# Attention on one core: the values matmuls between a transpose and a run of scores go behind the run

## What is computed

```python
cq = rms_norm(hidden_states @ w_qa.T, q_a_ln_w)
q = (cq @ w_qb.T)            # per head: 128 numbers, and 64 more with a rotary embedding
ckv_l = rms_norm(ckv[..., :KVLR], kv_a_ln_w)
scores = jnp.einsum('bhqd,bhkd->bhqk', q_full, k_full) * scale
scores = jnp.where(causal, -jnp.inf, scores)
attn = jax.nn.softmax(scores.astype(jnp.float32), axis=-1)
out = jnp.einsum('bhqk,bhkd->bhqd', attn, v)
return out @ w_o.T
```

## Time and profile before

| | before |
|---|---|
| median of 3 runs | 1726.22 us (1725.79 to 1726.46) |
| the profiled execution, its time | 1726.31 us |
| its span | 1724.6 us |
| attention loop in it | 99.4 to 1262 us |
| PE busy | 91% of the span |
| DVE busy | 69% |
| ACT busy | 59% |
| mean granted clock of PE | 0.972 of full speed |

### The profile page before, as it was taken

How to read it: one execution, slowest core, us unless ns; L and a number is a source line. 1 busy time by engine, 2 the same in 40 slices (tenths; PEclk the granted TensorE clock), 3 DMA queues, 4 the chain that set the end, 5 groups by cost and what they waited for, 6 DMA issues and landing times. The chain is left out here.

```text
span 1724.6 us, 38029 instructions
## 1 busy us (share of the span) xinstructions
PE 1571.8 (91%) x14452; PEld 1328.2 (77%) x14452; DVE 1184.3 (69%) x2472; ACT 1021.2 (59%) x2009; POOL 307.3 (18%) x752
## 2 busy tenths in 40 slices
PE   5679999999999899999999999999938999988997
PEld 3458877788888778888888888888826878866886
DVE  3347777777777677788778778778755547476564
ACT  2336665666666566667667667667624455555573
POOL 4411111112111211121211121121010002020231
PEclk8789999999999999999999999999968999999999
DMA  7000000000000000000000000000012100000000
GB/s 217 1 1 2 2 2 1 2 2 1 2 2 2 2 2 2 1 2 2 2 2 2 2 2 2 2 2 2 2 40 73 49 1 1 1 28 13 1 25 25
DMA packets 27524, 22.47 MB, mean 13 GB/s; under 512 B 9660, under 2 KB 25148, under 8 KB 27220
## 3 DMA queue, kind: packets, MB, share of 16 engines
q1 hardware_dynamic: 27348, 20.05, 4.1%
HBM read 17.95 MB, written 2.10 MB: 12 GB/s over the span
## 5 line engine op out<-in xcount | busy, mean ns | idle before, releaser
L783 ACT ACTIVATE pT_hi<-pT 128x512 f16<-128x512 f32 (+3 forms) x640 | 341.5, 534 | 303.6 <-PE pT L701 302.2
L904 DVE TENSOR_TENSOR pT_lo<-pT,pT_hi 128x512 f16<-128x512 f32 (+3 forms) x640 | 387.8, 607 | 148.5 <-ACT pT_hi L783 141.6
L772 ACT ACTIVATE pr<-pS,nmx 128x512 f32<-128x512 f32 (+3 forms) x640 | 401.0, 627 | 25.8 <-DVE nmx L895 24.0
L892 DVE TENSOR_REDUCE cmx<-pS 128x1 f32<-128x512 f32 x576 | 339.2, 617 | 64.0 <-PE pS L688 59.0
L701 PE MATMUL pT<-ident,pr 128*128 128x128 f32 x2176 | 347.3, 276 | 16.4 <-DVE pT_lo L904 15.1
L701 PEld LDWEIGHTS pT<-ident,pr 128*128 128x128 f32 x2176 | 251.9, 140 | 48.7 <-ACT pr L772 24.5
L743 PE MATMUL pO<-c_hi,pT_hi 128*128 128x65 f16 x2176 | 265.6, 194 | 18.5 <-DVE O L922 17.8
L683 PE MATMUL pS<-lT_hi,qT_hi 128*128 128x512 f32 (+2 forms) x640 | 265.5, 415 | 3.1 <-ACT pr L772 3.1
L744 PE MATMUL pO<-c_lo,pT_hi 128*128 128x65 f16 x2176 | 266.4, 193 | 0.0
L745 PE MATMUL pO<-c_hi,pT_lo 128*128 128x65 f16 x2176 | 263.7, 192 | 0.0
L688 PE MATMUL pS<-lT_hi,qT_lo 128*128 128x512 f32 (+2 forms) x640 | 255.8, 400 | 0.0
(11 more groups left out here) (268 smaller groups left out, 2484.6 us busy)
## 6 DMA issues: line engine op xcount, KB each, us to landing
X<-in_x SPq DMA_DIRECT2D x4, 512.0 KB, 6.8
wo<-in_w_o SPq DMA_DIRECT2D x1, 2048.0 KB, 10.9
out<-X SPq DMA_DIRECT2D x8, 256.0 KB, 2.0
raw<-in_wd SPq DMA_DIRECT2D x14, 128.0 KB, 2.1
raw<-in_wg SPq DMA_DIRECT2D x13, 128.0 KB, 2.7
raw<-in_wu SPq DMA_DIRECT2D x13, 128.0 KB, 2.7
wqn<-in_w_qn SPq DMA_DIRECT2D x1, 1536.0 KB, 16.1
raw<-in_qg SPq DMA_DIRECT2D x6, 128.0 KB, 2.5
```

Source lines behind the costliest of these rows:

```text
L772: act.activation(pr[:, at % RING, 0:n * P], pS[at % 4][:, 0:n * P], ACT.Exp, bias=nmx[:, p % 4:p % 4 + 1]).then_inc(sem("exped"), 1)
L783: act.activation(pT_hi[:, a % 4, 0:chunk[a][2] * P], src, ACT.Copy).then_inc(sem("t_hi"), 1)
L892: ch.inc(dve.tensor_reduce(cmx[:, p % 2, c:c + 1], pS[at % 4][:, 0:n * P], AX.X, ALU.max))
L904: dve.tensor_tensor(pT_lo[:, a % 4, 0:w], src, pT_hi[:, a % 4, 0:w], ALU.subtract).then_inc(sem("t_lo"), 1)
```

## The change

Eleven lines are put in behind the making of the list. They look for `probs`, `values`, `scores` in this order, and put the `values` behind the whole run of `scores` that follows.

```diff
+                n = 0
+                while n + 2 < len(plan):
+                    if plan[n][0] == "probs" and plan[n + 1][0] == "values" and plan[n + 2][0] == "scores":
+                        end = n + 2
+                        while plan[end][0] == "scores":
+                            end += 1
+                        plan.insert(end, plan[n + 1])
+                        plan.pop(n + 1)
+                        n = end
+                    n += 1
```

## The result

The changed kernel takes 1766.88 us (median of 4 runs, 1763.06 to 1767.62) against 1726.01 for the kernel before in the same runs: ratio 1.0241, interval 1.0227 to 1.0255, 41 us slower. The forecast was 1757, slower; the measured time lies 1.1 us inside the end of its range, 1768.

The account below looks back on a forecast made before the run. The prediction took PE as the bound in the attention loop's second half (busy 510.98 of 520.00 us). Its terms, 37 + 2 - 6 - 2 = +31 us on 1726, gave 1757 us; own range 1745 to 1767, stated range 1737 to 1768.

Parts of the forecast that it names:

- The late division: At 24 group ends DVE does `o_out` after the eviction and maxima, so PE's next first values wait: +37 us.
- Borders: Spacing between kinds of matmul on PE: 0.04 us gained per move away from group ends, -6 us in all.
- early scores: Moved-past scores, asked for about 0.45 us earlier, wait on PE for the exponential four chunks back: +2 us.
- Absorbed: Some new waits fall where PE would have waited anyway, for an eviction or the next tile's transposes: -2 us.
- A: Rival: DVE reaches `o_out` quickly at the 24 ends, 0.64 us per wait, 15 us, giving 1735 us; chance 0.12.
- B: Rival: earlier scores shrink PE's 48 us of first-half idle time, down to 1709 us; chance of faster 0.04.
- C: Rival: late PE restarts empty DVE and ACT, 0.5 us more at each of 24 ends, 1769 to 1785 us; chance 0.10.

Follow-up runs that it names:

- e1: The change without its 24 moves at group ends (194 moves stay), against the kernel before: 1721.16 us, ratio 0.9972.
- e4: Only the change's 12 moves at the ends of odd groups, against the kernel before: 1750.68 us, ratio 1.0146.
- e9: Order of before, but at 28 first-half group ends the last values stand ahead of the preceding run of scores, against the kernel before: 1735.09 us, ratio 1.0031.

## Why the prediction was right, and what it missed

**The late division, +37 us: right.** It measured 38.1. Place by place: 1.94 worked out and 1.93 measured at group 37, 0.86 and 0.85 at group 38, 1.65 and 1.72 at group 61, 1.70 and 1.74 at group 62. The step that mattered, that the eviction waits for ACT and so the division had sat in a hole of DVE's, is seen in the trace as the 0.65 us idle ahead of the eviction at 814.95.

**Borders, -6, and early scores, +2: right in sum, in part by luck.** The 194 moves alone shorten the loop by 3.7 us, where I had 4. The borders are as worked out: transposes to scores 0.03 (813.11 is 0.39 behind the first of four transposes, three of them 0.11 apart), scores to values 0.24 (813.66 to 813.90), which no row of before had. The early scores are as worked out too: 2 us in e1, at three places with 0.5 and three with 0.2. The split was different from mine. The first half kept 4.2 us, but 2.8 of them show as shorter waits for the division, which the sum has nowhere, so the agreement with 107 x 0.04 says little. The second half should have gained 87 x 0.04 = 3.5, less the 2 for early scores, and came out 0.5 longer; for that 2 us I have no cause.

**Absorbed, -2: right.** The change and e1 have the same order but for the 24 ends, and their loops differ by 44.6 us (1203.1 and 1158.5). 38.0 of these are waits for the division. From one group end to the next, with those waits taken off, the six stretches with a fall are 8.4 us longer. Two of them, behind groups 35 and 43, would be 0.4 us shorter each without it, as e4 shows, so the falls themselves cost 9.2. What is left is 44.6 - 38.0 - 9.2, so 2.6 us of other waits vanished behind the new ones. The kernel with even ends alone absorbs 0.7 of its 15.5 us.

**What was missing: the clock.** Each fall costs 1.5 to 1.6 us: 14 of the 18 measure so between two group ends, as at group 45 in e4, and the four behind groups 35 and 43 measure 1.1 to 1.2, because there 0.4 us of another wait went away at the same time. The six of the change are the 9.2 us. So the loop's 40.9 us are 38.0 + 9.2 - 2.6 - 3.7. I had no term for the clock, and it is nearly all of the distance between 1757 and 1766.88. I had looked at the mean clock of the halves, which only says that no wait of the old size had brought it down.

**The rivals.** A (short waits) is refuted by the 38.1 us. The measure of slack that the prediction took from the Trainium skill (Perfetto Trace Analysis, Identifying the Most-Contended Engine), by which the weight loads' 86% leave room for waits, is not borne out here: of 38.0 us of new waits 2.6 vanished, and of 15.5 in the kernel with even ends 0.7. That page of the Trainium skill says of matmul busy time that it is no good measure of how close one is to the peak, and not, as the prediction has it, that it overstates. B (early scores pay) is half of a small truth: the moves gave 4 us, not 31, and the early scores themselves cost 2. C came nearest in its number, not in its mechanism: the waits did breed something, a slow restart, by the clock and not by empty queues.

## What to carry to other kernels

When a step is moved on the engine that is the bound, look at what the other engines do at the same entry of the list: here PE waited 38 us more, and 26 of them came from DVE's division going behind other work, at the odd ends behind an eviction that was itself waiting. Price such a place by starts, from the last thing that the division's queue really waits for; this gave each of the four worked places to 0.07 us. And before a wait is taken away, ask whether its engine is the bound there: moving the last values early removed 22 us of waits and brought 28 us of others.

## What the hardware showed that I had not expected

A wait of TensorE of 1.9 to 2.3 us, in a part of the kernel in which it was busy for 98% of the time before (510.98 of 520 us), was followed in 18 cases by 3.4 us at 1.2 GHz in place of 2.4, at 1.5 to 1.6 us each. In 22 cases of the same length, in the same four kernels, it was not, and 44 waits of 0.8 to 1.9 us at such ends never were. Two waits of about 1 us in short succession were followed by it twice, in e9. Why one wait is followed by it and the next is not stays open.
